# ScalarE's order in layer 0's cross attention: casts and copies of transposes of pair n-2 ahead of the exponents of pair n

## What is computed

```python
ci = rms_norm(hidden_states, ln_post_cross_w)
cq = heads(ci @ cq_w, NH, CHD)                 # 16 heads of width 16
ck, cv = jnp.split(encoder_outputs @ ckv_w, 2, axis=-1)
ck, cv = (heads(ck, NH, CHD), heads(cv, NH, CHD))
scores = jnp.einsum('bhqd,bhkd->bhqk', q * scale, k)
p = jax.nn.softmax(scores, axis=-1)
cctx = jnp.einsum('bhqk,bhkd->bhqd', p, v)
hidden_states = hidden_states + cctx @ cdense_w
```

## Time and profile before

| | us |
|---|---|
| runs: median of 3 (lowest, highest) | 2050.86 (2050.78, 2052.18) |
| profiled execution, its own time | 2044.05 |
| its span | 2042.2 |
| TensorE busy | 1924.6 (94%) |
| VectorE busy | 1112.1 (54%) |
| ScalarE busy | 829.5 (41%) |
| GpSimd busy | 886.0 (43%) |

### The profile page before, as it was taken

The page is one execution under the profiler, slowest core; times in us unless marked ns, Lnnn a source line. Parts: engine busy times, 40 slices in busy tenths (PEclk is TensorE's granted clock), DMA queues, the critical chain, the costliest instruction groups (busy, mean ns, idle before and its releaser), DMA issues.

```text
span 2042.2 us, 35472 instructions
## 1 busy us (share of the span) xinstructions
PE 1924.6 (94%) x12620; PEld 1646.9 (81%) x12620; DVE 1112.1 (54%) x2663; ACT 829.5 (41%) x2198; POOL 886.0 (43%) x1037
## 2 busy tenths in 40 slices
PE   4999979997999999999999999998979999999998
PEld 3876767776899988889888879995458989888997
DVE  6777875665452552446676545222374767655422
ACT  2026527775211121246666523222235666652321
POOL 3340322240688999742121238850044212103884
PEclk9999988988999999999999999999989999999999
DMA  3110100010233333310000123322221000001332
GB/s 126 42 57 2 40 15 17 30 43 13 83 104 108 111 116 120 108 34 18 10 24 13 41 89 93 114 83 87 69 80 34 18 10 24 13 1 42 103 111 81
DMA packets 38190, 118.88 MB, mean 58 GB/s; under 512 B 6168, under 2 KB 10264, under 8 KB 38016
## 3 DMA queue, kind: packets, MB, share of 16 engines
q1 hardware_dynamic: 31408, 107.92, 17.1%
q10 hardware_dynamic: 6608, 8.68, 1.4%
HBM read 114.75 MB, written 1.84 MB: 57 GB/s over the span
## 4 chain that ended last, share of the span: by engine, by line
PE 82%; DVE 8%; POOL 4%; issue 2%; ACT 2%; DMA 1%; DVEq 0%; SPq 0%; ACTq 0%; POOLq 0%
PE psum L565 15%; PE psum L567 14%; PE psum L566 14%; PE psum L787 7%; PE psum L798 6%; PE psum L845 5%; PE psum L558 4%; PE psum L685 4%; PE psum L687 4%; PE psum L686 4%; POOL wl L1694 2%; DVE rstd L1255 1%; DVE xc L1270 1%; DVE total L1241 1%; PE psum L859 1%
## 5 line engine op out<-in xcount | busy, mean ns | idle before, releaser
L1694 POOL TENSOR_TENSOR wl<-raw,wh 128x256 fp32r<-128x256 f32 x656 | 518.7, 822 | 13.7
L565 PE MATMUL psum<-nh,wh 128*128 128x448 f32 x904 | 349.8, 387 | 15.2 <-DVEq L1470 7.8
L1686 POOL TENSOR_SCALAR wh<-raw 128x1024 fp32r<-128x1024 f32 x164 | 185.3, 1130 | 400.9 <-PE psum L567 164.0
L566 PE MATMUL psum<-nl,wh 128*128 128x448 f32 x904 | 337.7, 374 | 0.0
L567 PE MATMUL psum<-nh,wl 128*128 128x448 f32 x904 | 337.1, 373 | 0.0
L1044 ACT ACTIVATE probs_t<-masked_t,nmin 112x375 f32<-112x375 f32 (+1 forms) x384 | 202.6, 529 | 109.9 <-DVE nmin L1373 109.9
L1542 DVE TENSOR_TENSOR hid_l<-scr,hid_h 128x448 fp32r<-128x448 f32 x108 | 92.9, 860 | 228.6 <-ACT hid_h L1122 227.9
L565 PEld LDWEIGHTS psum<-nh,wh 128*128 128x128 f32 x904 | 175.7, 194 | 38.1 <-issue 13.3
L798 PE MATMUL psum<-cst,probs_t 112*125 112x112 f32 (+1 forms) x1304 | 190.2, 276 | 13.6 <-ACT probsT_t L1064 13.2
L798 PEld LDWEIGHTS psum<-cst,probs_t 112*125 112x125 f32 (+1 forms) x1304 | 167.7, 186 | 36.5 <-ACT probs_t L1044 12.2
L1373 DVE CUSTOM_DVE_ANT_0 masked_t<-psum,maskf 112x375 f32<-112x375 f32 x256 | 129.8, 545 | 117.0 <-PE psum L787 116.3
(11 more groups left out here) (182 smaller groups left out, 3857.0 us busy)
## 6 DMA issues: line engine op xcount, KB each, us to landing
raw<-in_walls SPq DMA_DIRECT2D x183, 512.0 KB, 3.5
raw<-in_ctxF SPq DMA_DIRECT2D x24, 375.0 KB, 3.0
ctxb<-in_ctxF ACTq DMA_DIRECT2D x8, 375.0 KB, 3.8
ctxt<-in_ctxK ACTq DMA_DIRECT2D x8, 375.0 KB
x<-in_xT ACTq DMA_DIRECT2D x2, 896.0 KB, 11.3
outT<-x SPq DMA_DIRECT2D x2, 896.0 KB, 5.1
mask<-in_kmask ACTq DMA_DIRECT2D x16, 41.0 KB, 2.6
vself<-in_tt SPq DMA_DIRECT2D x1, 448.0 KB, 6.5
```

The source lines that it names most:

```text
L565: nc.tensor.matmul(out, ah, bh, start=(i == 0), stop=False)
L566: nc.tensor.matmul(out, ah, bl, start=False, stop=False)
L1686: nc.gpsimd.tensor_scalar(high, src, 1.0, 1.0, ALU.mult, ALU.mult).then_inc(split_h, 1)
L1694: last = nc.gpsimd.tensor_tensor(low[cut], src[cut], high[cut].bitcast(F32), ALU.subtract)
```

## The change

In ScalarE's `attention`, the loop over the exponents of a pair becomes a function `exponents`. For all attentions but `att_c0` it is called where the loop stood. For `att_c0` it is called at the end of the iteration, behind the casts of iteration n and the copies of pair n-2. No instruction is added or left out, and no wait is changed.

```diff
+            def exponents(a, heads):
+                for s in heads:
+                    act.wait_ge(a.maxed, s + 1)
+                    if s >= NPROB:
+                        act.wait_ge(a.turned, s - NPROB + 1)
...
             def attention(a):
                 pairs = a.steps // a.pair
                 for n in range(pairs + LAG):
                     heads = range(a.pair * n, a.pair * n + a.pair)
-                    for s in heads if n < pairs else ():
-                        act.wait_ge(a.maxed, s + 1)
...
+                    if n < pairs and a is not att_c0:
+                        exponents(a, heads)
                     for s in heads if n < pairs else ():
                         for unit in projected(a, s):
                             project(a, *unit)
...
+                    if n < pairs and a is att_c0:
+                        exponents(a, heads)
```

More of the change, by code:

```diff
@@ L1028, in project @@
                 nc.scalar.copy(dst.rearrange("p c n -> p (c n)"), bank[0:KEYS, 0:w]).then_inc(emptied["act"], 1)
+            def exponents(a, heads):
[3 more added lines that the diff above has]
+                        act.wait_ge(a.turned, s - NPROB + 1)
+                    total = rsum[:, s % NPROB:s % NPROB + 1]
+                    if a is att_c0:
+                        total = rsum8[:, s % 8:s % 8 + 1]
+                        if s >= 8:
+                            act.wait_ge(a.recip, s // 4 - 1)
+                    src = s_bank(a, s)[:, 0:a.nk] if a.mask is None else masked_s[s % NMASK][:, 0:a.nk]
+                    nc.scalar.activation(probs[s % NPROB][:, 0:a.nk], src, ACT.Exp, scale=-1.0,
+                                         bias=nmin[:, s % NPROB:s % NPROB + 1],
+                                         accum_out=total).then_inc(a.exped, 1)
             def attention(a):
```

## The result

The changed kernel takes 2036.72 us (median of 5 runs, 2031.68 to 2041.80), the kernel before, run beside it, 2050.78 (5 runs). The ratio is 0.9935, 95% interval 0.9917 to 0.9954. In a second set, with more runs, it is 2036.40 (9 runs) against 2046.01 (24 runs), ratio 0.9947 (0.9928 to 0.9967). So the kernel is faster by some 10 us, and not by the 5.7 that I forecast; 2036.72 lies under the range of 2038.5 to 2051.5.

The account below looks back on a forecast made before the run. TensorE, waiting for copies in layer 0's cross attention, nearly bounds the kernel; start 0.3, seven batches 3.8, last batch 1.0 and end 0.6 give 5.7 us off, 2045.2 us predicted, range 2038.5 to 2051.5.

Parts of the forecast that it names:

- What bounds the kernel: Layer 0's cross attention: TensorE nearly the bound, busy 19.85 of 21.03 us a batch, idling for copies of transposes.
- The wait that goes: TensorE's transposes no longer wait for copies queued behind exponents; waits of 0.77 and 0.41 us a batch go.
- The wait that comes: Exponents queue behind a second copy that waits for the weighing, forming a loop between scores of 4.12 us.
- The quads: Stretches of four heads in a batch: gains 0.59, 0.21, 0 and loss 0.25, together 0.55 us a batch.
- The start: First pair: exponent's table load moves behind the first K cast; bounds 1.3 lost to 1.3 won, 0.3 won taken.
- The last batch: Last batch's quads without projections become two loops of 4.12 us; gain 1.0 us taken.
- the end: The attention's last transposes wait 1.47 us for copies; gain between 0 and 1.5, 0.6 us taken.
- Behind the section: Code after the attention, including the MLP: follows TensorE, so the gain counts in full.
- rival 4: Clock: batch 5's stretch at TensorE's lower level may go, stay or come twice, 4.1 us either way; no chance of its own.
- rival 1: Attention batches: nothing takes the removed wait's place, all waits go, 10 us gained, 2040.9; chance 0.15.
- The base: Starting time: profiled execution of 2044.05 us taken as 6.8 us under the median 2050.86, same difference kept for the forecast.
- Rivals 2 and 3: Longer new loop in the quads: gain eaten, about 2049 to 2050.5, chance 0.22; or late exponents, 2054.2, chance 0.08.

Follow-up runs that it names:

- before_a: The kernel before, unaltered, profiled again; 177.89 us from the first scores to the attention's last weighing.
- before_b: The kernel before, unaltered, profiled once more; 178.25 us from the first scores to the attention's last weighing.
- bfill2: The kernel before, plus unread filling matmuls in TensorE's waits, three in iteration 2 and one in iteration 5 of each batch; 2043.06 us, ratio 0.9978 to before.
- ring6: The changed kernel with six buffers instead of five in this attention's ring of transposed heads; 2030.13 us.
- after_wait: The changed kernel with one wait a batch put back, ahead of TensorE's transposes in iteration 2; 2053.19 us.
- bfill: The kernel before, plus unread filling matmuls in TensorE's waits, five in iteration 2 and three in iteration 5 of each batch; 2048.00 us.
- ring4: The changed kernel with four buffers instead of five in this attention's ring of transposed heads; 2042.57 us.
- after2: The changed kernel again, unaltered, against the kernel before in new rounds; 2036.40 us.

## Why the prediction was wrong

Point by point, in its own order.

*What bounds the kernel* was right. *The wait that goes* went: no copy holds the transposes in the batches. *The wait that comes* was right in place and size: the second copy waits for the weighing, exponents stand behind it, and scores wait for them. The quads came out at 4.23, 5.18, 6.02 and 5.19 us (401.72, 405.95, 411.13, 417.15, 422.34), where I had 4.12, 5.16, 6.00 and 5.20. One term was mis-sized, from the second exponent to the scores, and only in the quad without projections: 0.81 instead of 0.71, while with K it is 0.72 (410.41 to 411.13). So 0.41 us a batch and not 0.55, 2.9 us in seven and not 3.8.

*The start* failed in its sign: I took 0.3 won, and S(0) to S(2) took 1.06 us more. The choice between the bounds was a guess that the earlier cast would win; by S(4) only 0.3 of it had come back, 10.58 from S(0) instead of 9.79. *The last batch* gave 0.84 where I took 1.0, the end 1.19 where I took 0.6, but 0.5 of that is the clock's fall in the profile of before; against the 9.69 us of before_a and before_b it is 0.7. *Behind the section* was right, nothing is given back.

The sum of the order is thus about 3.5 us, where I had 5.7. By itself that would have made the result slower than forecast, not faster.

**The step that failed is rival 4.** I read the stretch at the lower clock in batch 5, argued that TensorE's order there is that of the batch before, and concluded that it might go, stay or come twice whatever the case. So it stood in the sum at nothing. The first half holds, the conclusion doesn't. The fall needs something that the change removes: the wait of 0.77 us in iteration 2. Every batch has it, and behind one of these waits in an execution (three profiles of three) the clock falls; without them it doesn't from 340 to 470 us, in six profiles of kernels with the new order and two with the old order and the waits filled, and with one put back it falls again. The profile of before alone held the clue. In its timeline of PE, the first group that is longer than its like (1.04 instead of 0.89 us, and 1.35 instead of 0.78 for the next L845) is the one behind that wait:

```profile
423.73 1.04 PE L798 MATMUL psum<-cst,probs_t 112*125 112x112 f32 x6 [0.76 <-ACT probsT_t L1064]
424.56 0.39 PE L816 MATMUL psum<-cst,rexp 112*128 112x112 f32 x1
424.89 1.35 PE L845 MATMUL psum<-probsT_t,v 125*32 125x112 f32 x24
```

It was worth 3.6 us (bfill2, interval 1.4 to 7.4) to 4.1 us (25.10 against 21.03), on one side only. As a certain gain it would have put the forecast at 2041.1 and the range's low end, rival 1 with all of it, at 2036.8.

*The base* added to it. I placed the forecast by the median of three runs, 2050.86, and took the profiled execution at 2044.05 for one that lay low. Over 24, 17 and 23 runs the median is 2046.0 to 2046.8, so the profiled execution was an ordinary one. So some 4 us of the first difference of 14 are chance in the three to five runs of before. From 2044.05 the forecast was 2038.4, and the profiled execution of the changed kernel took 2036.72. That this is near is luck: the order was put 2.2 us too high and the clock's fall 4.1 too low.

*Rivals 1 to 3.* Rival 1 (nothing takes the wait's place) is what ring6 shows: 19.69 us a batch, which needs the sixth buffer. Rivals 2 and 3 rested on a longer loop; it was 0.1 longer in one quad of a batch and 0.02 or less in the others.

*What stays open.* Of the 9.6 us between the medians the order gives about 3.5 and the fall in the batches about 4; some 2 are left. Nor is it shown why the clock falls at one of the seven equal waits, in batch 5 or 6 of before and in two batches of after_wait, and not at the others. The length of a wait alone doesn't decide it: ring6 has one of 0.64 us ahead of 464.88 us, without a fall there. The mean clock says that there is more to find: span times (1 - clock) is 56 us for before, 51 for bfill2 and 46 for the changed kernel, while the fall in the batches accounts for 5 (0.04 x 130). The other 5 between bfill2 and the changed kernel lie somewhere else in the program and differ from profile to profile; no run here ties them to the change.

## What to carry to other kernels

A wait of well under a microsecond on an engine that is nearly full can cost more than its own length, if TensorE's clock falls behind it: before calling a stretch at the lower clock chance, read which row is its first, and whether other batches have the same wait. Filling the wait with matmuls whose result nobody reads is a cheap test of that, as long as they fill no more than the wait (bfill2) and don't lengthen the batch (bfill). When work is reordered on an in-order engine, look for the wait in the moved neighbours that cost nothing because nothing urgent stood behind it; here one more buffer in its ring was worth 6.3 us, more than the reordering's own 3.5.

## What the runs showed of the hardware that I had not expected

- The granted clock of TensorE fell while it was busy in 19.85 of 21.03 us, less than 1 us behind the end of a wait of 0.64 to 0.79 us (before, before_a, before_b, after_wait: 5 falls). Waits of 0.20 to 0.30 us, three in a batch (changed kernel), and of 0.48 and 0.57 us (ring4) brought no fall in the profiles from 340 to 470 us, and neither did most waits of 0.77 us.
- One such fall costs 4.1 us here (25.1 against 21.0 us a batch).
- Behind a table load of 1.28 us the exponent began after 0.02 us (changed kernel).
- The runs of before beside after2 spread over 2040 to 2054 us with the mean granted clock at 0.978 to 0.968.
